# Rotary embedding in a two-layer attention kernel: partner rows by projection or by a row shuffle

## The chip, the cores and the metric

The kernel runs on one core of a Trainium2 chip. The metric is the device time of one execution in microseconds (us); the shown time is the median of three runs. The engines are TensorE (PE, with its weight loads as PEld), VectorE (DVE), ScalarE (ACT), GpSimd (POOL) and SyncE (SP), which issues the transfers.

## What is computed

Two layers over 64 sequences of 128 rows and 128 features, with 16 heads of 8 features. The first layer has a self-attention, a cross-attention to 77 context rows and an MLP; the second has one more cross-attention. Only the queries and keys of the self-attention are rotated:

```python
def _apply_rope(t, cos, sin):
    t1, t2 = jnp.split(t, 2, axis=-1)
    rot = jnp.concatenate([-t2, t1], axis=-1)
    return t * cos + rot * sin
...
t = (h @ qkv_W).reshape(b, n, 3, H, HD)
q, k, v = (t[:, :, 0], t[:, :, 1], t[:, :, 2])
return (_apply_rope(q, cos, sin), _apply_rope(k, cos, sin), v)
...
s = jnp.einsum('bqhd,bkhd->bhqk', q, k) * scale
a = jax.nn.softmax(s, axis=-1)
```

The first and the second 64 rows of a sequence carry the same positions, so a table of cosines or sines is 128 features by 64 columns. A feature's partner is the one four places further on in its head of eight, or four places back.

## The kernel before

Features lie on the partitions and rows (tokens) on the columns. Four sequences make a group of 512 columns; each of the three attentions has 16 groups, and a group has eight units (four sequences, two halves of the heads). The program is one long list of slots, a unit to a slot. On each engine the order within a slot is written out by hand; the class `Plan` gives the slots of the jobs that use the two PSUM banks `ps_pj`: projections ("q", "k", "v"), centring ("c") and mean square ("m") of the layer norm, and the output projection ("o"). A job's bank alternates with its place in the list, and the job two places before it must have been read first (`free_bank`).

In a slot of the self-attention PE does this, in order: at every second slot the transposition of the split maxima (L520, waits for POOL's L871); the mask products into both score banks (L491, wait for the row maxima of the slot before, L637, and for the exponentials, L815); the scores in natural order for the unit six ahead (L506); the transposed scores (L534); the value products of the unit before (L555); then the jobs that `Plan` calls late. L555 waits, in a slot with a transposition L520, for the copy L645 that DVE makes of what L520 wrote.

DVE in a slot: first the jobs of the slot before (the reads of `ps_pj`, L622 for the projections), then at every second slot the copy `mt` of the transposed maxima (L645), then the row maxima `negmax` over 1024 columns of PSUM (L637), then at every second slot five instructions that read out the values (L656 to L663; the last is a row shuffle over 128 columns).

Call b the slot in which PE projects the queries of a self-attention group. The jobs are q in slot b, the rotated query qr in b+1, k and the next group's c in b+2, the rotated key kr in b+3, m in b+4, o in b+5, v in b+6. qr and kr multiply by `wrot`, in which the four-feature halves of each head's columns of `wqkv` change places; the sine table carries the signs. DVE multiplies q by `cosq` and qr by `sinq` (the softmax scale is in both), one slot after PE each; k and kr go the same way with `cos` and `sin`. Both products of a pair lie in `part`; POOL adds them into `whole` (L885). From there ACT rounds the high part to bf16 (L750), POOL takes the rest and repeats the high part (L890, L891), and two more steps make the remaining bf16 parts (L755 on ACT, L897 and L898 on POOL), which SP sends to `stacks`.

In the set-up, ACT makes `wrot` with four copies (L175) and DVE makes `cosq` and `sinq` (L132, L133); PE's first instruction waits for `sinq`. Ahead of the first unit there are 28 slots of start-up, in which PE also transposes the incoming groups (L413, L416), each of which waits for its transfer.

## Time and profile before

| | |
|---|---|
| median of 3 runs | 1246.61 us (1243.92 to 1249.29) |
| the profiled execution | 1245.41 us, of which the span is 1243.6 us |
| mean granted TensorE clock | 0.96 of full speed |
| PE busy | 1070.5 us (86%) |
| DVE / ACT / POOL busy | 833.2 / 848.6 / 846.2 us (67% / 68% / 68%) |
| self-attention, from its first row maxima to its last output | about 97 to 475 us |

PE is the busiest engine, but the others stand at two thirds, and the four hand work to each other within every slot. So the shares alone do not tell which one sets the pace in a slot: that is read from the waits, in the order of time. In the rows, "[0.49 <-PE ps_nat L506]" behind an instruction means that its engine sat idle for 0.49 us before it and that PE's L506 ended that.

### The profile page before, as it was taken

The numbers are of one execution on the slowest core, as the hardware profiler recorded it, in microseconds if no ns is written. First come the engines' busy times: TensorE is split into PE (matmuls) and PEld (weight loads), VectorE is DVE, ScalarE is ACT, GpSimd is POOL, SyncE is SP. The second block draws the span as 40 slices with busy tenths as digits, with TensorE's granted clock in tenths as the row PEclk, the third lists the DMA queues.
The fourth block names the chain that finished last, engine by engine and source line by source line (L and its number), as shares of the span: only waits on it lengthen the run. The fifth ranks groups of instructions, "written<-read, shape, count | busy, mean of one in ns | idle before, by whom it ended". The sixth has DMA issues, their size and how long they took to land.

```text
span 1243.6 us, 42372 instructions
## 1 busy us (share of the span) xinstructions
PE 1070.5 (86%) x16230; PEld 612.6 (49%) x16230; DVE 833.2 (67%) x2198; ACT 848.6 (68%) x1527; POOL 846.2 (68%) x1799
## 2 busy tenths in 40 slices
PE   0677888898898988888898788999998999999987
PEld 0543444444444444555555455444443566666665
DVE  3336777887787877878888775223224687888875
ACT  0234666666656666888888777778876787888765
POOL 0048767767767866887788643466878787888742
PEclk9978999999999999999999987999999899999988
DMA  3266554564654554656666660000023566776761
GB/s 102 70 168 119 102 97 86 101 107 77 105 103 86 99 93 77 107 100 99 115 108 103 104 108 6 0 1 1 17 38 57 87 119 120 126 128 123 122 119 38
DMA packets 165242, 109.92 MB, mean 88 GB/s; under 512 B 42778, under 2 KB 164787, under 8 KB 165043
## 3 DMA queue, kind: packets, MB, share of 16 engines
q1 hardware_dynamic: 165042, 107.22, 48.2%
q8 instruction: 131, 2.15, 0.7%
q14 instruction: 69, 0.56, 0.1%
HBM read 9.08 MB, written 4.19 MB: 11 GB/s over the span
## 4 chain that ended last, share of the span: by engine, by line
PE 44%; POOL 12%; issue 11%; ACT 10%; SPq 9%; DMA 5%; DVE 5%; POOLq 0%; ACTq 0%; DVEq 0%
PE ps_po L555 7%; SPq L989 7%; ACT p L815 5%; PE ps_st L534 5%; PE ps_nat L506 4%; PE ps_st L567 4%; PE ps_pj L436 4%; PE ps_po L576 4%; PE ps_pj L453 4%; PE ps_pj L431 3%; DMA stacks<-mt 3%; DVE negmax L637 2%; PE ps_pj L444 2%; POOL whole L890 2%; POOL parts L891 2%
## 5 line engine op out<-in xcount | busy, mean ns | idle before, releaser
L637 DVE TENSOR_REDUCE negmax<-ps_nat 128x8 f32<-128x616 f32 (+1 forms) x384 | 359.8, 937 | 92.8 <-PE ps_nat L506 85.0
L815 ACT ACTIVATE p<-ps_st 128x1024 f32<-128x1024 f32 (+1 forms) x256 | 260.7, 1018 | 193.6 <-PE ps_st L534 192.5
L555 PE MATMUL ps_po<-p,vz 77*32 77x128 f32 (+1 forms) x6144 | 258.9, 288 | 3.5 <-ACT p L815 2.1
L534 PE MATMUL ps_st<-stacks 64*77 64x128 bf16 (+1 forms) x3072 | 157.9, 224 | 24.3 <-DMA stacks<-mt 13.1
L815 ACT ACTIVATE p<-ps_st,key_bias 77x1024 f32<-77x1024 f32 x128 | 141.8, 1108 | 50.9 <-PE ps_st L534 49.0
L555 PEld LDWEIGHTS ps_po<-p,vz 77*32 77x32 f32 (+1 forms) x6144 | 150.9, 112 | 43.4 <-issue 7.5
L506 PE MATMUL ps_nat<-stacks 64*128 64x77 bf16 (+1 forms) x3072 | 135.0, 210 | 26.4 <-issue 14.6
L879 POOL TENSOR_TENSOR ot<-vv,den 128x128 f32<-128x128 f32 x192 | 87.3, 455 | 102.5 <-ACT den L803 97.3
L506 PEld LDWEIGHTS ps_nat<-stacks 64*128 64x128 bf16 x3072 | 79.3, 97 | 151.9 <-issue 140.0
L890 POOL TENSOR_TENSOR whole<-whole,parts 128x512 f32<-128x512 f32 x96 | 98.6, 1027 | 57.1 <-ACT parts L750 57.0
L534 PEld LDWEIGHTS ps_st<-stacks 64*77 64x77 bf16 (+1 forms) x3072 | 107.5, 111 | 35.5 <-ACT p L815 27.9
L917 POOL TENSOR_TENSOR ht<-xc,nrm 128x512 f32<-128x512 f32 x48 | 60.9, 1268 | 75.8 <-ACT nrm L786 58.5
L645 DVE COPY mt<-ps_po 128x128 bf16<-128x128 bf16 x192 | 42.4, 221 | 100.7 <-PE ps_po L520 99.6
L898 POOL TENSOR_TENSOR parts<-whole,parts 128x512 bf16<-128x512 f32 x96 | 98.6, 1027 | 0.0
L891 POOL COPY parts<-parts 128x1024 bf16<-128x1024 bf16 x96 | 88.5, 922 | 0.0
L922 POOL TENSOR_SCALAR ht<-ht,mod 128x128 f32<-128x128 f32 x192 | 83.2, 448 | 5.0
L436 PE MATMUL ps_pj<-nrm,mean 128*128 128x512 f32 (+1 forms) x160 | 80.4, 599 | 5.2 <-ACT nrm L784 4.6
L685 DVE COPY xc<-ps_pj 128x512 f32<-128x512 f32 (+1 forms) x64 | 39.5, 631 | 51.5 <-PE ps_pj L431 51.2
L520 PE MATMUL ps_po<-eye_bf,nm 128*128 128x128 bf16 x192 | 43.8, 228 | 35.0 <-POOL nm L871 33.9
L656 DVE TENSOR_SCALAR dd<-ps_po,lower 128x128 f32<-128x128 f32 x192 | 65.6, 342 | 11.6 <-PE ps_po L555 11.6
L491 PE MATMUL ps_nat<-rolled,eye_bf 32*32 32x512 bf16 x1024 | 55.8, 389 | 17.4 <-ACT p L815 12.0
L431 PE MATMUL ps_pj<-xt,centre 128*128 128x512 f32 x128 | 70.0, 629 | 0.7 <-DVE xc L685 0.4
(146 smaller groups left out, 2139.8 us busy)
## 6 DMA issues: line engine op xcount, KB each, us to landing
stacks<-parts SPq DMA_DIRECT2D x512, 128.0 KB, 3.2
stacks<-parts SPq DMA_DIRECT2D x256, 77.0 KB, 2.8
stacks<-mt SPq DMA_DIRECT2D x192, 32.0 KB, 2.4
p<-in_x_dram SPq DMA_DIRECT2D x16, 256.0 KB
out_dram<-part SPq DMA_DIRECT2D x16, 256.0 KB, 2.3
p<-in_ctx_dram SPq DMA_DIRECT2D x16, 154.0 KB
stacks<-in_L_xcond_adaLN_W_dram SPq DMA_DIRECT2D x1, 576.0 KB
w<-in_L_xcond_mlp_W_dram SPq DMA_DIRECT2D x2, 256.0 KB
```

Of the source, the lines that this page charges most:

```text
L431: t.matmul(bank_of(job)[:, 0:w], c.centre[:], src[:, at:at + w], start=True, stop=True).then_inc(pj_full, 1)
L436: t.matmul(bank_of(job)[:, 0:w], c.mean[:], c.nrm[:, plan.norms[job[1]] % 3, 0:w], start=True, stop=True).then_inc(pj_full, 1)
L506: m = t.matmul(c.ps_nat[h][:, nk * g:nk * g + nk], qst[half(h), par, at, S * j:S * j + S], kst[half(h), par, at, nk * j:nk * j + nk], star ...
L534: m = t.matmul(c.ps_st[h][0:nk, S * g:S * g + S], kst[half(h), par, at, nk * j:nk * j + nk], qst[half(h), par, at, S * j:S * j + S], start ...
L555: m = t.matmul(c.ps_po[step % 2][32 * g:32 * g + 32, S * p:S * p + S], c.vz[0:nk, i % 2, step % G, g, at:at + 32], c.p[0:nk, hh, S * g:S * ...
L637: v.tensor_reduce(c.negmax[:, step % 2, :].rearrange("p (h q g) -> p h q g", h=2, q=2)[:, :, p, :], c.nat_pair[:].rearrange("p (h n) -> p ...
L815: a.activation(c.p[0:nk, 2 * p:2 * p + 2, :].rearrange("p h n -> p (h n)"), c.st_pair[0:nk, :], ACT.Exp, bias=bias).then_inc(exped, 1)
L879: p.tensor_tensor(c.ot[:, i % 2, S * j:S * j + S], c.vv[:, step % 2, :], c.den[:, step % 2, :], ALU.mult).then_inc(out_ready, 1)
L890: p.tensor_tensor(c.whole[:, x, w], c.whole[:, x, w], parts[:, hi[0], w], ALU.subtract).then_inc(rest, 1)
L891: p.tensor_copy(parts[:, hi[1]:hi[2] + 1:hi[2] - hi[1], w], parts[:, hi[0]:hi[0] + 1, w].broadcast_to([128, 2, width(i, x)]))
L898: p.tensor_tensor(parts[:, LOW[x], w], c.whole[:, x, w], parts[:, md[0], w], ALU.subtract).then_inc(split[x], 1)
L989: sp.dma_start(st[:, i % 3, t, 0:w], c.parts[16 * t:16 * t + 16, x, 6 * (i % 2):6 * (i % 2) + 8, 0:w]).then_inc(stacked[x][p][i % 3], 16)
```

## The change

The projections qr and kr are taken out, with `wrot` and ACT's four copies. DVE now reads the bank of q twice in one go: once times the cosine into `part`, once times the sine into `gated` (a tile that is otherwise used by the MLP). Then, behind a wait for that second product, it shuffles the rows of `gated` into the second half of `part`, so that each row gets the product of its partner. For this the sine table itself must be in shuffled order, which is one more shuffle (and one wait) in the set-up. POOL's addition waits for the shuffle instead of for the second projection's product.

```diff
+PARTNER_ROWS = [r ^ (HD // 2) for r in range(32)]
...
-            load(c.sin[:], ins["sin"])
+            load(c.sin_in[:], ins["sin"])
...
             v.tensor_scalar(c.cosq[:], c.cos[:], SCALE, None, ALU.mult)
+            v.stream_shuffle(c.sin[:], c.sin_in[:], PARTNER_ROWS).then_inc(shuffled, 1)
+            dve.wait_ge(shuffled, 1)
             v.tensor_scalar(c.sinq[:], c.sin[:], SCALE, None, ALU.mult).then_inc(ready, 1)
...
-            for x in range(2):
-                src = c.wqkv[:, D * x:D * x + D].rearrange("p (h t e) -> p h t e", t=2, e=4)
-                dst = c.wrot[:, x, :].rearrange("p (h t e) -> p h t e", t=2, e=4)
-                for t in range(2):
-                    a.activation(dst[:, :, t, :], src[:, :, 1 - t, :], ACT.Copy)
...
-            for kind, r in ((("q", 0), ("qr", 1), ("k", 2), ("kr", 3)) if i < NG else (("q", -1), ("k", 1))):
+            for kind, r in ((("q", 0), ("k", 2)) if i < NG else (("q", -1), ("k", 1))):
...
                 if a == 0:
-                    r = len(kind) - 1
                     if 2 * i + x > 0:
                         dve.wait_ge(turned, 2 * i + x)
-                    table = ((c.cosq, c.sinq), (c.cos, c.sin))[x][r]
-                    v.tensor_tensor(c.part[:, r, :].rearrange("p (r n) -> p r n", n=64),
-                                    bank[:].rearrange("p (r n) -> p r n", n=64),
-                                    table[:].unsqueeze(1).broadcast_to([128, 8, 64]), ALU.mult).then_inc(taken, 1)
+                    blocks = lambda tile: tile.rearrange("p (r n) -> p r n", n=64)
+                    for table, dst in zip(((c.cosq, c.sinq), (c.cos, c.sin))[x], (c.part[:, 0, :], c.gated[:, x, :])):
+                        m = v.tensor_tensor(blocks(dst), blocks(bank[:]), table[:].unsqueeze(1).broadcast_to([128, 8, 64]), ALU.mult)
+                    m.then_inc(taken, 1)
+                    dve.wait_ge(taken, plan.taken[job])
+                    v.stream_shuffle(c.part[:, 1, :], c.gated[:, x, :], PARTNER_ROWS).then_inc(rotated, 1)
...
             def turn(i, x):
-                pool.wait_ge(taken, plan.taken["qk"[x] + "r", i])
+                pool.wait_ge(rotated, 2 * i + x + 1)
```

How this moves instructions, first on PE. The place is slots b and b+1 of a self-attention group: `wqkv` with `ht` is the projection q, `wrot` the projection qr. Before:

```order
L555 MATMUL ps_po<-p,vz 32x128 x8
L453 MATMUL ps_pj<-ht,wqkv 128x512
L520 MATMUL ps_po<-eye_bf,nm 128x128
L491 MATMUL ps_nat<-rolled,eye_bf 32x512 x2
L491 MATMUL ps_st<-rolled,eye_bf 32x512 x2
...
L506 MATMUL ps_nat<-stacks 128x128 x8
L534 MATMUL ps_st<-stacks 128x128 x8
L555 MATMUL ps_po<-p,vz 32x128 x8
L453 MATMUL ps_pj<-ht,wrot 128x512
L491 MATMUL ps_nat<-rolled,eye_bf 32x512 x2
```

And now (line numbers are one or two lower):

```order
L554 MATMUL ps_po<-p,vz 32x128 x8
L452 MATMUL ps_pj<-ht,wqkv 128x512
L519 MATMUL ps_po<-eye_bf,nm 128x128
L490 MATMUL ps_nat<-rolled,eye_bf 32x512 x2
L490 MATMUL ps_st<-rolled,eye_bf 32x512 x2
...
L505 MATMUL ps_nat<-stacks 128x128 x8
L533 MATMUL ps_st<-stacks 128x128 x8
L554 MATMUL ps_po<-p,vz 32x128 x8
L490 MATMUL ps_nat<-rolled,eye_bf 32x512 x2
```

The value products of slot b+1 are now followed at once by the mask products of slot b+2; slot b+3 changes in the same way.

On DVE, slots b+1 to b+3 of a group. Before:

```order
L622 TENSOR_TENSOR part<-ps_pj,cosq 128x512
L645 COPY mt<-ps_po 128x128
L637 TENSOR_REDUCE negmax<-ps_nat 128x2x4
...
L663 STREAM_SHUFFLE den<-dd 128x128
L622 TENSOR_TENSOR part<-ps_pj,sinq 128x512
L637 TENSOR_REDUCE negmax<-ps_nat 128x2x4
L622 TENSOR_TENSOR part<-ps_pj,cos 128x512
L645 COPY mt<-ps_po 128x128
L637 TENSOR_REDUCE negmax<-ps_nat 128x2x4
```

Now:

```order
L621 TENSOR_TENSOR part<-ps_pj,cosq 128x512
L621 TENSOR_TENSOR gated<-ps_pj,sinq 128x512
L624 STREAM_SHUFFLE part<-gated 128x512
L645 COPY mt<-ps_po 128x128
L637 TENSOR_REDUCE negmax<-ps_nat 128x2x4
...
L663 STREAM_SHUFFLE den<-dd 128x128
L637 TENSOR_REDUCE negmax<-ps_nat 128x2x4
L621 TENSOR_TENSOR part<-ps_pj,cos 128x512
L621 TENSOR_TENSOR gated<-ps_pj,sin 128x512
L624 STREAM_SHUFFLE part<-gated 128x512
L645 COPY mt<-ps_po 128x128
L637 TENSOR_REDUCE negmax<-ps_nat 128x2x4
```

The sine product has moved forward by one slot, and it and the shuffle now stand ahead of the copy `mt` and of the row maxima of slot b+1 (and again of b+3); slots b+2 and b+4 have lost a product.

## Rows read from the trace of the kernel before

**Rows 1.** The page's first part: busy time, share of span, instructions, by engine.
```profile
PE 1070.5 (86%) x16230; PEld 612.6 (49%) x16230; DVE 833.2 (67%) x2198; ACT 848.6 (68%) x1527; POOL 846.2 (68%) x1799
```

**Rows 2.** Busy time by stretch: length, then PE, PEld, DVE, ACT, POOL, clock, DMA.
```profile
240.00:300.00 60.00, 52.84 (x1048) 28.09 (x1050) 47.31 (x111) 36.38 (x69) 45.42 (x91) 1.00 0.59 103
```

**Rows 3.** Timeline, POOL: L890 for the queries, groups 4 and 15 of 16.
```profile
135.78 1.16 POOL L890 TENSOR_TENSOR whole<-whole,parts 128x512 f32<-128x512 f32 x1 [3.96 <-ACT parts L750]
...
398.61 1.16 POOL L890 TENSOR_TENSOR whole<-whole,parts 128x512 f32<-128x512 f32 x1 [3.96 <-ACT parts L750]
```

**Rows 4.** Timeline, PE, one period: start, duration, engine, line, what, idle before.
```profile
245.42 0.23 PE L520 MATMUL ps_po<-eye_bf,nm 128*128 128x128 bf16 x1 [0.36 <-POOL nm L871]
...
246.49 0.64 PE L555 MATMUL ps_po<-p,vz 128*32 128x128 f32 x16
247.07 1.12 PE L453 MATMUL ps_pj<-ht,wrot 128*128 128x512 f32 x2
248.12 0.39 PE L491 MATMUL ps_nat<-rolled,eye_bf 32*32 32x512 bf16 x2
...
253.08 1.12 PE L453 MATMUL ps_pj<-ht,wrot 128*128 128x512 f32 x2
...
258.42 0.23 PE L520 MATMUL ps_po<-eye_bf,nm 128*128 128x128 bf16 x1 [1.67 <-POOL nm L871]
```

**Rows 5.** Timeline, the other engines, the same period.
```profile
245.09 0.69 DVE L622 TENSOR_TENSOR part<-ps_pj,cosq 128x512 f32<-128x512 f32 x1 [0.46 <-PE ps_pj L453]
...
245.70 0.21 DVE L645 COPY mt<-ps_po 128x128 bf16<-128x128 bf16 x1
...
246.41 1.22 DVE L637 TENSOR_REDUCE negmax<-ps_nat 128x8 f32<-128x1024 f32 x1 [0.49 <-PE ps_nat L506]
...
249.55 1.27 POOL L885 TENSOR_TENSOR whole<-part 128x512 f32<-128x512 f32 x1 [0.80 <-DVE part L622]
...
255.24 1.16 POOL L890 TENSOR_TENSOR whole<-whole,parts 128x512 f32<-128x512 f32 x1 [3.96 <-ACT parts L750]
```

**Rows 6.** By line: count, then ns least/median/most, first and last start, forms.
```profile
L663 DVE STREAM_SHUFFLE den<-dd x192: 289/294/302, 123.6 to 1235.9; 128x128 f32<-128x128 f32 x192
...
L685 DVE COPY xc<-ps_pj x64: 466/680/692, 401.0 to 1153.3; 128x512 f32<-128x512 f32 x48, 128x308 f32<-128x308 f32 x16
...
L164 DVE COPY bp_rows<-ps_pj x1: 292/292/292, 44.9 to 44.9; 128x128 f32<-128x128 f32 x1
```

**Rows 7.** Timeline, set-up.
```profile
33.47 0.27 PE L184 MATMUL ps_pj<-eye,stacks 25*128 25x25 f32 x1 [33.47 <-DVE sinq L133]
...
34.71 0.19 DVE L139 TENSOR_SCALAR stacks<-stacks 128x64 f32<-128x64 f32 x1 [0.32 <-ACT stacks L177]
...
34.94 0.55 DVE L141 RECIPROCAL stacks<-stacks 128x64 f32<-128x64 f32 x1
```

**Rows 8.** Timeline, DVE and PE's weight loads, slots b+1 and b+2 of the last group.
```profile
413.57 0.69 DVE L622 TENSOR_TENSOR part<-ps_pj,cosq 128x512 f32<-128x512 f32 x1 [0.60 <-PE ps_pj L453]
...
414.35 1.23 DVE L637 TENSOR_REDUCE negmax<-ps_nat 128x8 f32<-128x1024 f32 x1
...
416.16 0.09 PEld L491 LDWEIGHTS ps_nat<-rolled,eye_bf 32*32 32x32 bf16 x2 [0.76 <-DVE negmax L637]
```

**Rows 9.** Timeline, PE, start-up.
```profile
66.93 2.00 PE L453 MATMUL ps_pj<-ht,wrot 128*128 128x512 f32 x2
...
79.70 0.66 PE L413 MATMUL ps_st<-eye,p 128*128 128x128 f32 x4 [2.83 <-DMA p<-in_ctx_dram]
...
105.67 2.07 PE L453 MATMUL ps_pj<-ht,wrot 128*128 128x512 f32 x2
```

**Rows 10.** A timeline row of PE, then two stretches (columns as in Rows 2).
```profile
465.60 0.23 PE L520 MATMUL ps_po<-eye_bf,nm 128*128 128x128 bf16 x1 [1.67 <-POOL nm L871]
...
465.00:468.00 3.00, 2.18 (x49) 1.30 (x50) 1.63 (x4) 1.02 (x1) 2.87 (x6) 0.77 0.71 129
552.00:555.00 3.00, 3.00 (x26) 1.32 (x30) 1.89 (x7) 1.96 (x4) 1.94 (x5) 0.50 0.44 69
```

More of the change, by code:

```diff
@@ L50, in setup_phase @@
                                                  s("su_silu_d"), s("su_copied"))
-    headed = s("su_headed")
+    headed, shuffled = s("su_headed"), s("su_shuffled")
     made, masks, mask_ps = s("su_made"), s("su_masks"), s("su_mask_ps")
@@ L322, in by_dve @@
     def by_dve(self, job):
-        return job[0] in ("q", "qr", "k", "kr", "o") or job[0] == "c" and not self.copied_by_act(job[1])
+        return job[0] in ("q", "k", "o") or job[0] == "c" and not self.copied_by_act(job[1])
     @staticmethod
@@ L336, in main_phase @@
     rooted, multiplied, applied = s("rooted"), s("multiplied"), s("applied")
+    rotated = s("rotated")
     turned, high, rest, mid = s("turned"), s("high"), s("rest"), s("mid")
@@ L362, in main_phase @@
     width = lambda i, x: NT if x == 0 else G * keys(i)
-    weights = [{"q": c.wqkv[:, 0:D], "k": c.wqkv[:, D:2 * D], "v": c.wqkv[:, 2 * D:3 * D], "qr": c.wrot[:, 0, :], "kr": c.wrot[:, 1, :]},
+    weights = [{"q": c.wqkv[:, 0:D], "k": c.wqkv[:, D:2 * D], "v": c.wqkv[:, 2 * D:3 * D]},
                {"q": c.w0[:, 0, :], "k": c.w0[:, 1, :], "v": c.w0[:, 2, :]},
@@ L1044, in two_layers @@
         c.wqkv = sb("wqkv", [D, 3 * D])
-        c.wrot = sb("wrot", [D, 2, D])
+        c.sin_in = sb("sin_in", [128, 64])
         c.w0 = sb("w0", [D, 3, D])
```

## The prediction

> **What bounds the kernel now.** The page first: PE is the busiest engine, the others stand at two thirds [rows 1]. That does not say that PE sets the pace, so the stretch in which the change lives comes next: between 240 and 300 us PE is busy 52.84 of 60 us at full clock, DVE 47.31, POOL 45.42 [rows 2]. Nobody is full; the pace is a cycle through several engines. How regular it is shows in POOL's L890: from the fourth to the fifteenth group it comes from 135.78 to 398.61 us, 11 periods of 23.89 us [rows 3]. So one period, followed link by link, gives the self-attention.
>
> I read the period around 245 us backwards from its longest PE wait. At 258.42 PE has waited 1.67 us for POOL's L871 (slot b+5) [rows 4]. POOL is late because L890 started only at 255.24, after 3.96 us of waiting for ACT's L750 [rows 5]; that stands behind the exponentials of slot b+3, which wait for PE's scores of that slot. PE reaches slot b+3 without any wait once the mask products of b+2 have started at 248.12, and these start when the projection qr (247.07) has left PE [rows 4]. So up to b+3 the start of PE's work is what counts, and behind b+3 PE has 1.67 us in hand.
>
> **The change, part by part.** All times are those of the period in [rows 4, 5].
>
> *Taking qr off PE (slot b+1).* Without it PE could start the mask products of b+2 as soon as the row maxima of b+1 are there: they start at 246.41, take 1.22 and end at 247.63; PE follows about 0.06 later, at 247.69. Before it was 248.12. The most that this removal can give is 0.43 us a group, not the 1.05 us that the projection holds PE.
>
> *What DVE does instead.* q is there at 245.09, as before. A 512-column product releases the next instruction after 0.61 (245.09 to 245.70), so the sine product runs from 245.70 to 246.39. Then comes the wait for its own result. Instructions that don't wait start about 0.08 before the end of the one before; where DVE waits for its own result, as from L139 (ends 34.90) to L141 (34.94), it starts 0.04 after the end [rows 7]. So the shuffle starts at 246.43.
>
> How long is a 128x512 shuffle? The trace has only 128x128: 0.294 [rows 6]. A copy grows from 0.292 at 128 columns to 0.692 at 512 [rows 6], 0.400 for 384 columns; with the same growth the shuffle takes 0.69. Its ends are 0.29 (width costs nothing) and 4 x 0.294 = 1.18 (no fixed part). I take 0.69, since the two instructions cost the same at 128 columns. The shuffle ends at 247.12.
>
> The copy `mt` then runs from 247.04 to 247.25, where it was at 245.70, and the row maxima from 247.17 to 248.39. Two engines wait for these. PE's value products L555 wait for `mt` and start at 247.31 instead of 246.49; they end in time. The mask products of b+2 wait for the maxima and start at 248.45 instead of 248.12. **So slot b+1 costs 0.33 us a group more, not 0.43 less.** With a shuffle of 0.29 it would be 0.07 less than before, with 1.18 it would be 0.82 more.
>
> By the Trainium skill, "VectorE: DVE Perf Modes", the perf-mode tier table, a row shuffle has only the 1x rate, about 2400 ns at 2048 columns; a quarter of that is an estimate of 0.60 us here. With it the cost would be 0.24 a group instead of 0.33. The same page, "The DRAIN you can't avoid", says that a semaphore between Vector instructions costs nothing extra. The trace disagrees (0.08 before the end against 0.04 after it); by the page the cost would be lower by 0.12 a group.
>
> *Slot b+2.* DVE has lost a product there, which had hidden behind PE. POOL's addition L885 waited 0.80 for qr's product [rows 5]; now the shuffle is early, but POOL first splits the maxima that come 0.76 later (247.63 to 248.39), takes 1.06 for that, and starts L885 at 249.45 instead of 249.55. Nothing waits for the 0.10.
>
> *Slots b+3 and b+4: kr.* k is ready at 251.11 (values from 249.37, 0.58 for them, 1.16 for the projection as for q). Cosine product, sine product, wait and shuffle take 2.03, so `mt` is copied at 253.06, the value products start at 253.33, the maxima end at 254.41, and the mask products of b+4 start at 254.47 instead of 254.13 (before: behind kr, 253.08 plus 1.05). That is 0.34 late, which is no more than the 0.33 brought along: the loss in this slot is covered by kr's going. And behind it lies PE's wait of 1.67 [rows 4]. If that cover were gone, its full price is about what b+1 costs.
>
> *Period.* L750, L890 and the transposition in b+5 all come 0.33 later; b+5 to b+8 have no edit. Twelve groups (the fourth to the fifteenth): 12 x 0.33 = **+4.0**.
>
> *The last group* has no next group to centre, and DVE runs closer behind PE: its maxima start 0.78 after the q product (413.57 to 414.35) without a wait [rows 8], where in the period there are 1.32. They now start at 415.65 and end at 416.87, and PE's next slot starts at 416.93 instead of 416.16 [rows 8]: **+0.8**.
>
> *Set-up.* PE's first instruction waits for `sinq` [rows 7]. Ahead of it stand one shuffle of 64 columns (0.23 by the same growth) and a wait (0.04): **+0.3**. ACT's four copies hid beside this.
>
> *Start-up.* Six rotated projections lie here, some at the half clock, 2.00 and 2.07 long [rows 9]. Together they are at most 6 x 2.07 = 12.4, at least nothing. Most of what they free is given back to the transfers: PE waits for the input again and again, 2.83 us at 79.70 [rows 9], and each input is requested only when an earlier one has been transposed. Only the one at 105.67 has no such wait behind it, and the shuffles take part of that back. I take half of that one: **-1.0**.
>
> *Sum:* 4.0 + 0.8 + 0.3 - 1.0 = +4.1 on the profiled execution's 1245.4: 1249.5. That execution lies 1.2 below the median of the runs, so for a median I say **1250.7**.
>
> **The rivals.**
>
> *The clock falls more often (slower).* PE gets emptier: in b+1 it now idles some 0.8 ahead of the value products and 0.6 behind them, and in b+3 and b+4 again 0.5 and 0.6, with the 1.67 us still there. In the twelve periods no such gap lowered the clock, but the same gap at 465.60 was followed by a granted clock of 0.77 and then 0.67 (the 1.2 GHz level in part of the stretch), and in the cross-attention there are stretches of 3 us wholly at 0.50, that is at 1.2 GHz [rows 10]. In 3 us at half clock and 3.00 busy, PE does 1.5 us less. Two to six falls more: +3 to +9, 1254 to 1260. Against it: the gap itself gets no longer.
>
> *The cover in b+3 fails (slower).* If DVE's late maxima in b+3 reach the exponentials or POOL, each group pays about 0.33 twice: +4 to +5 more, 1255. It decides from 1.67 us of lateness in b+4, and I count 0.34. Weak.
>
> *The start-up gives more (faster).* If no transfer waits for what PE no longer does, the six projections are worth up to 12.4 and half of them, 6.2, would give 1245.4 + 1.2 + 5.1 - 6.2 = 1245.5; with a short shuffle as well (0.29: -0.07 instead of +0.33 a group) 1240.7. By the full 12.4 and the forecast shuffle it is 1239.3, which is faster. Against it: the waits for transfers.
>
> *The edit does nothing.* If PE's 1.05 and DVE's addition cancelled in every slot, 1246.6. It takes a shuffle of about 0.36, half of what I take.
>
> **How the numbers follow.** Forecast (1247.5 to 1253.5): 0.50. More clock falls: 0.27. Cover fails, or a shuffle towards 1.18 (12 x 0.49 = +5.9): 0.08. No effect: 0.08. Start-up gain: 0.07. The range leaves out the far ends of the first rival and the larger start-up gains: 1244 to 1260. A measurement of this kernel can tell 0.5% from no change, 6.2 us: slower begins at 1252.8. Slower: most of the falls (0.24), the failing cover (0.07) and the forecast's upper edge (0.08), 0.39. Faster: 0.05. Same: 0.56.
>
> **What would show it.** In the changed profile: STREAM_SHUFFLE 128x512 at 0.69; the sine product 0.61 behind the cosine; PE's mask products in b+2 waiting for L637 instead of following a projection; L890's period at 24.2; PE's wait for L871 in b+5 still near 1.6; L885 no longer waiting for DVE; PE's clock at 1.00 between 120 and 450 us. A period of 23.9 or less, or one of 24.6, makes the sum wrong; so does a start of the periods (135.8) that moves by more than 2 us.

## The result and the profile after

The changed kernel takes **1273.99 us** (median of 4 runs, 1267.11 to 1279.98), the kernel before in the same session 1246.92 (1243.92 to 1249.29): ratio 1.0217, 95% interval 1.0159 to 1.0274. It is slower by 2.2%, 27 us, where +4.1 had been forecast, and it lies outside the range. The interval is clear of no change, but it doesn't say whether the loss is more than 2%. The profiled execution took 1279.98 us with a span of 1278.2, 34.6 more than the span of before; it is the slowest of the four.

The first part of the page of after, to be held against [rows 1]:

```profile
PE 1069.3 (84%) x16166; PEld 618.9 (48%) x16166; DVE 853.4 (67%) x2264; ACT 848.8 (66%) x1523; POOL 849.0 (66%) x1799
```

PE has lost 64 matmuls and hardly any busy time (1069.3 for 1070.5). The projections that went were paid back by slower ones elsewhere: the mean clock fell from 0.960 to 0.932. So the place to look is the clock by stage. Stretches of before, then of after (length, busy time and instructions of PE, PEld, DVE, ACT, POOL, then PE's granted clock, DMA share, GB/s). In both they are: the start-up, up to the fourth group's L890; the 11 periods; the last groups of the self-attention; the cross-attention and what overlaps it; the rest:

```profile
0.00:135.80 135.80, 80.14 (x742) 47.82 (x746) 62.38 (x124) 37.92 (x75) 49.67 (x84) 0.92 0.49 116
135.80:398.60 262.80, 229.34 (x4516) 122.73 (x4512) 204.99 (x481) 165.47 (x309) 196.58 (x385) 1.00 0.55 96
398.60:443.00 44.40, 38.30 (x737) 20.32 (x729) 34.90 (x81) 29.31 (x55) 37.03 (x74) 1.00 0.52 96
443.00:723.80 280.80, 245.08 (x4478) 143.94 (x4482) 226.30 (x655) 223.34 (x407) 212.63 (x499) 0.97 0.60 101
723.80:1243.60 519.80, 477.64 (x5777) 277.81 (x5777) 304.63 (x860) 392.52 (x683) 350.31 (x761) 0.94 0.40 70
```
```profile
0.00:137.90 137.90, 75.08 (x726) 47.44 (x730) 67.46 (x142) 37.24 (x71) 49.70 (x83) 0.89 0.48 113
137.90:417.30 279.40, 223.01 (x4472) 123.84 (x4468) 218.32 (x526) 166.13 (x309) 196.97 (x386) 0.94 0.51 90
417.30:464.60 47.30, 38.98 (x733) 20.86 (x725) 36.05 (x85) 29.26 (x55) 37.19 (x73) 0.93 0.51 90
464.60:751.80 287.20, 250.03 (x4478) 145.71 (x4482) 226.36 (x655) 223.52 (x407) 213.72 (x500) 0.95 0.59 99
751.80:1278.20 526.40, 482.19 (x5777) 281.02 (x5773) 305.18 (x860) 392.69 (x683) 351.46 (x761) 0.93 0.39 69
```

Taken from L890 to L890, the difference of 34.6 is +2.2 in the start-up, +16.5 in the 11 periods, +3.0 in the last groups, +6.3 in the cross-attention and +6.6 in the rest. In the first three the change has its edits; the code of the last two is the same in both kernels.

**One period, as forecast.** The timeline of after, slot b+1 of a group in which the clock stayed at 1.00 (start, duration, engine, line, what, idle before); the rows answer to [rows 4, 5]:

```profile
177.91 0.69 DVE L621 TENSOR_TENSOR part<-ps_pj,cosq 128x512 f32<-128x512 f32 x1 [0.46 <-PE ps_pj L452]
178.51 0.68 DVE L621 TENSOR_TENSOR gated<-ps_pj,sinq 128x512 f32<-128x512 f32 x1
179.24 0.72 DVE L624 STREAM_SHUFFLE part<-gated 128x512 f32<-128x512 f32 x1
179.85 0.21 DVE L645 COPY mt<-ps_po 128x128 bf16<-128x128 bf16 x1
179.97 1.22 DVE L637 TENSOR_REDUCE negmax<-ps_nat 128x8 f32<-128x1024 f32 x1
180.21 0.64 PE L554 MATMUL ps_po<-p,vz 128*32 128x128 f32 x16 [0.79 <-DVE mt L645]
181.25 0.09 PEld L490 LDWEIGHTS ps_nat<-rolled,eye_bf 32*32 32x32 bf16 x2 [0.66 <-DVE negmax L637]
182.47 1.27 POOL L885 TENSOR_TENSOR whole<-part 128x512 f32<-128x512 f32 x1
191.57 0.23 PE L519 MATMUL ps_po<-eye_bf,nm 128*128 128x128 bf16 x1 [1.70 <-POOL nm L871]
```

Everything stands where the working put it. Counted from the cosine product, the sine product starts 0.60 later, `mt` 1.94, the maxima 2.06, the mask products 3.34 (worked out: 0.61, 1.95, 2.08, 3.36). L885 waits for nobody, and the long wait in b+5 is 1.70.

**Three periods.** The same for POOL's L890 (queries) of four groups in a row, as in [rows 3], and what stands in the last of the three periods: two waits of PE with a row of PE between them, and four stretches of 3 us (columns as above):

```profile
188.37 1.16 POOL L890 TENSOR_TENSOR whole<-whole,parts 128x512 f32<-128x512 f32 x1 [3.96 <-ACT parts L750]
212.59 1.16 POOL L890 TENSOR_TENSOR whole<-whole,parts 128x512 f32<-128x512 f32 x1 [3.96 <-ACT parts L750]
236.82 1.16 POOL L890 TENSOR_TENSOR whole<-whole,parts 128x512 f32<-128x512 f32 x1 [3.96 <-ACT parts L750]
263.75 1.16 POOL L890 TENSOR_TENSOR whole<-whole,parts 128x512 f32<-128x512 f32 x1 [5.10 <-ACT parts L750]
```
```profile
240.02 0.23 PE L519 MATMUL ps_po<-eye_bf,nm 128*128 128x128 bf16 x1 [1.69 <-POOL nm L871]
251.54 0.22 PE L519 MATMUL ps_po<-eye_bf,nm 128*128 128x128 bf16 x1
254.04 0.65 PE L554 MATMUL ps_po<-p,vz 128*32 128x128 f32 x16 [1.36 <-DVE mt L645]
```
```profile
240.00:243.00 3.00, 2.98 (x51) 1.46 (x51) 2.21 (x6) 1.74 (x3) 3.00 (x4) 0.80 0.05 11
243.00:246.00 3.00, 3.00 (x51) 1.60 (x51) 2.79 (x9) 1.76 (x3) 2.67 (x7) 0.63 0.41 62
253.00:256.00 3.00, 1.56 (x44) 1.10 (x46) 2.96 (x11) 0.77 (x1) 0.68 (x4) 0.91 0.18 39
256.00:259.00 3.00, 3.00 (x28) 1.65 (x25) 1.40 (x4) 1.53 (x3) 1.84 (x3) 0.52 0.86 158
```

The first two periods are 24.22 and 24.23, and 24.22 had been forecast. The third is 26.93. In it PE waits 1.69 at 240.02, and from 241.8 to 245.1 it has the 1.2 GHz level; it waits 1.36 for `mt` at 254.04, and has 1.2 GHz again from 255.4 to 258.9. The second wait is a new one: it lies in the slot in which DVE now has the shuffle ahead of `mt`. It is longer here than the 0.79 of 180.21 although the clock is back at 1.00. The first fall has delayed PE, so POOL's L871 is now ready in time: at 251.54 PE doesn't wait for it, where it waits 0.39 one group earlier (226.72). PE so reaches the copy sooner, and DVE's way to the copy is as long as before (2.30 from the cosine product to L554, both times). The two falls cost 2.71 together, 1.36 each on the average. Of the 11 periods six have the forecast length, one costs 2.0 more and four cost 2.7 more: 11 x 0.33 = 3.6 for the lateness and 12.9 for the clock, 16.5 together.

**All runs, by their clock.** Each run comes with its mean granted clock. The 82 other runs of the kernel before that accompanied the experiments have 0.943 to 0.969, median 0.955 at a span of 1246.8; the time at half clock is twice the span times (1 - clock), 112 us in the median run. Over these 82 runs the span grows by 0.31 us for each us at half clock. The four of after have 0.932 to 0.943, median 0.936, 162 us at half clock: 50 us more, at 0.31 each 15.5. The median span is 25.4 longer; 4 to 5 of it are the forecast lateness, and the some 5 left are not placed. In after's 11 periods a us at half clock cost more, 0.38 (12.9 for 34). This is an estimate, from how the runs of before spread; by it the larger part of the loss is clock over the runs too, not only in the profiled one.

### The profile page after: what moved, and what is told of

Its sections match the earlier page's. It is cut to its first block, busy times and chain, and to the rows that moved or that the text cites. A ratio compares the mean times of both kernels' runs of the same rounds, so it can differ in the third digit from the quotient of the medians.

```text
span 1278.2 us, 42276 instructions
## 1 busy us (share of the span) xinstructions
PE 1069.3 (84%) x16166; PEld 618.9 (48%) x16166; DVE 853.4 (67%) x2264; ACT 848.8 (66%) x1523; POOL 849.0 (66%) x1799
## 4 chain that ended last, share of the span: by engine, by line
PE 48%; ACT 11%; issue 11%; SPq 8%; DVE 7%; POOL 6%; DMA 5%; POOLq 0%; DVEq 0%; ACTq 0%
PE ps_po L554 9%; ACT p L815 6%; SPq L989 6%; PE ps_st L533 5%; PE ps_nat L505 5%; PE ps_pj L452 4%; PE ps_st L566 4%; PE ps_pj L435 4%; PE ps_po L575 4%; PE ps_pj L430 4%; PE ps_pj L443 3%; DMA stacks<-mt 3%; DVE negmax L637 2%; PE ps_nat L490 2%; POOL whole L890 2%
## 5 line engine op out<-in xcount | busy, mean ns | idle before, releaser
L554 PE MATMUL ps_po<-p,vz 77*32 77x128 f32 (+1 forms) x6144 | 266.1, 294 | 23.7 <-DVE mt L645 22.3
L554 PEld LDWEIGHTS ps_po<-p,vz 77*32 77x32 f32 (+1 forms) x6144 | 155.6, 114 | 66.8 <-issue 24.5
L533 PE MATMUL ps_st<-stacks 64*77 64x128 bf16 (+1 forms) x3072 | 162.6, 228 | 25.7 <-DMA stacks<-mt 14.8
L505 PE MATMUL ps_nat<-stacks 64*128 64x77 bf16 (+1 forms) x3072 | 138.1, 213 | 27.2 <-issue 15.2
L890 POOL TENSOR_TENSOR whole<-whole,parts 128x512 f32<-128x512 f32 x96 | 98.7, 1028 | 68.1 <-ACT parts L750 67.9
L533 PEld LDWEIGHTS ps_st<-stacks 64*77 64x77 bf16 (+1 forms) x3072 | 111.0, 114 | 36.6 <-ACT p L815 23.5
L490 PE MATMUL ps_nat<-rolled,eye_bf 32*32 32x512 bf16 x1024 | 57.2, 402 | 29.6 <-DVE negmax L637 16.5
L865 POOL CAST nm<-negmax 128x16 bf16<-128x16 f32 x192 | 37.9, 197 | 53.2 <-DVE negmax L637 52.6
```

The source lines that it names most:

```text
L505: m = t.matmul(c.ps_nat[h][:, nk * g:nk * g + nk], qst[half(h), par, at, S * j:S * j + S], kst[half(h), par, at, nk * j:nk * j + nk], star ...
L533: m = t.matmul(c.ps_st[h][0:nk, S * g:S * g + S], kst[half(h), par, at, nk * j:nk * j + nk], qst[half(h), par, at, S * j:S * j + S], start ...
L554: m = t.matmul(c.ps_po[step % 2][32 * g:32 * g + 32, S * p:S * p + S], c.vz[0:nk, i % 2, step % G, g, at:at + 32], c.p[0:nk, hh, S * g:S * ...
L890: p.tensor_tensor(c.whole[:, x, w], c.whole[:, x, w], parts[:, hi[0], w], ALU.subtract).then_inc(rest, 1)
```

## The experiments

The theory: the change puts idle time of PE into b+1 and b+3 (ahead of and behind the value products), and with it the clock falls behind PE's longer waits. Rivals: the gap in b+5 alone does it (then filling b+1 and b+3 helps nothing); the shuffle's place ahead of the maxima does it; the changed spacing of the waits (the period) does it.

"Filling" means products that compute nothing that is used. They go into the PSUM bank of the job that comes next:

```diff
+            def fill(slot, place):
...
+                for _ in range(n[place]):
+                    t.matmul(bank_of(job)[:, 0:192], weights[0]["q"], ht(i)[:, 0:192], start=True, stop=True)
...
+                fill(slot, 0)
                 if val is not None:
                     values(val)
...
+                fill(slot, 1)
```

The table has all kernels: "falls" are the drops of the clock that begin between 120 and 430 us of the profiled execution (the 11 periods end at 395 to 417, so a fall can lie behind them), "11 periods" their length and clock in it; then come the median clock of all runs, the median time and the ratio to the runs of before on the same chip.

| kernel | period | falls | 11 periods | clock in them | clock, all runs | us | ratio (95%) |
|---|---|---|---|---|---|---|---|
| before (a second profile: c_before_again) | 23.89 | 0 (0) | 262.8 (262.9) | 1.00 | 0.955 | 1246.9 | 1 |
| after | 24.22 | 9 | 279.3 | 0.94 | 0.936 | 1274.0 | 1.022 (1.016 to 1.027) |
| a_fill13 | 24.27 | 1 | 267.7 | 0.99 | 0.948 | 1263.1 | 1.011 (1.004 to 1.019) |
| a_fillall | 24.26 | 0 | 266.6 | 1.00 | 0.954 | 1258.2 | 1.006 (1.003 to 1.010) |
| b_fillgap | 24.21 | 2 | 265.7 | 1.00 | 0.948 | 1262.7 | 1.012 (1.005 to 1.019) |
| a_noshuffle | 23.57 | 7 | 265.6 | 0.96 | 0.944 | 1256.6 | 1.005 (1.002 to 1.008) |
| a_late | 23.60 | 5 | 262.1 | 0.98 | 0.944 | 1256.8 | 1.004 (1.001 to 1.007) |
| b_latefill | 23.58 | 1 | 259.4 | 1.00 | 0.948 | 1253.1 | 1.005 (1.002 to 1.008) |
| b_longer | 24.75 | 4 | 273.4 | 0.98 | 0.950 | 1263.9 | 1.014 (1.007 to 1.021) |
| b_beforegap | 23.89 | 0 | 262.8 | 1.00 | 0.954 | 1251.2 | 1.003 (0.999 to 1.007) |
| c_before_delay | 24.16 | 5 | 267.7 | 0.97 | 0.952 | 1253.6 | 1.008 (1.005 to 1.010) |
| c_late_delay | 24.17 | 7 | 271.1 | 0.96 | 0.937 | 1266.2 | 1.018 (1.014 to 1.021) |
| d_late_delay1 | 23.89 | 1 | 263.1 | 0.99 | 0.952 | 1252.4 | 1.000 (0.997 to 1.004) |
| c_latefill_start | 23.58 | 0 | 259.6 | 1.00 | 0.960 | 1249.3 | 1.002 (0.999 to 1.005) |
| d_before_once | 23.89 | 0 | 262.9 | 1.00 | 0.953 | 1252.4 | 1.002 (0.999 to 1.005) |
| d_before_start | 23.89 | 0 | 262.9 | 1.00 | 0.962 | 1248.6 | 1.001 (0.997 to 1.004) |

### Filling PE's new idle time, and the old gap

a_fill13 is after with one product of 192 columns ahead of and one behind the value products in b+1 and b+3. a_fillall has three more at the end of b+4, ahead of the long wait. b_fillgap has only these three.

> The changed kernel, with small matrix products given back to TensorE where it now waits: in slots b+1 and b+3 of each self-attention group one product of 192 columns ahead of the value products and one behind them (32 x 2 products of about 0.4 us; their results are overwritten unread, the output is the same). Clock theory (most of the loss comes from the clock's falls, which the emptier TensorE brings on): the falls that follow slot b+1 go, those behind the 1.7 us wait in b+5 may stay; 1252 to 1262. Latency theory (the shuffle ahead of the copy mt and of the row maxima is what costs, and the falls only go with it): no gain, 1270 or more. Undisturbed periods 24.2 to 24.3 under both.

> As the run before, and in addition three products of 192 columns (about 1.2 us) behind the last job of slot b+4, that is in the 1.7 us for which TensorE waits for L871 in b+5 (for groups 1 to 14). Clock theory: hardly any fall is left between 120 and 450 us, periods of 24.2 to 24.4 throughout, 1246 to 1254. Latency theory: 1270 or more.

> The changed kernel with the wait of 1.7 us in b+5 filled alone (three products of 192 columns) and slots b+1 and b+3 left empty. Which of the empty places brings the falls: if the long wait is enough alone, no fall is left between 120 and 450 us and the time is that with everything filled, 1254 to 1260. If the emptiness of b+1 and b+3 brings them by itself, four or more are left, behind b+1: 1262 to 1270.

The 11 periods of the three, in this order:

```profile
139.40:407.20 267.80, 231.69 (x4560) 130.38 (x4564) 217.39 (x526) 165.56 (x309) 196.31 (x386) 0.99 0.54 94
```
```profile
137.60:404.20 266.60, 241.17 (x4622) 141.24 (x4621) 216.99 (x525) 165.49 (x308) 196.35 (x385) 1.00 0.54 95
```
```profile
137.90:403.60 265.70, 219.98 (x4538) 128.22 (x4534) 216.96 (x526) 165.46 (x309) 196.26 (x385) 1.00 0.54 95
```

With more for PE to do, each stretch is 12 to 14 us shorter than in after, and the clock is back. 266.6 is 11 x 24.22 = 266.4 and nothing else: the lateness that was forecast, without the clock. Either filling alone is nearly enough in the profiled execution (one fall left, and two, both of which begin behind the 11 periods), so neither gap is the sole cause. Over the runs, a_fillall brings the ratio from 1.022 down to 1.006, but its 1258.2 lies above the 1246 to 1254 that the clock theory had expected. The span of its profiled execution is 13.0 above that of before: 3.8 of it in the periods, 1.8 in the start-up, 0.8 in the last groups, and 6.6 in the cross-attention and the rest, whose code is the same. The other two stay at 1.011 and 1.012 with wide intervals (4 runs each); b_fillgap's profiled execution lost in the cross-attention (293.0 for before's 280.8), in code that no edit touches.

### The shuffle left out, and the shuffle behind the maxima

a_noshuffle leaves the shuffle out: POOL adds the sine product as it is, so the partner rows are the wrong ones. PE's work is that of after.

```diff
-                    for table, dst in zip(((c.cosq, c.sinq), (c.cos, c.sin))[x], (c.part[:, 0, :], c.gated[:, x, :])):
+                    for table, dst in zip(((c.cosq, c.sinq), (c.cos, c.sin))[x], (c.part[:, 0, :], c.part[:, 1, :])):
...
-                    dve.wait_ge(taken, plan.taken[job])
-                    v.stream_shuffle(c.part[:, 1, :], c.gated[:, x, :], PARTNER_ROWS).then_inc(rotated, 1)
...
-                pool.wait_ge(rotated, 2 * i + x + 1)
+                pool.wait_ge(taken, plan.taken["qk"[x], i])
```

a_late keeps it, with its wait, but issues it behind the row maxima of the slot:

```diff
                     maxima(unit_at(slot + AHEAD))
+                for job in coming:
+                    if job[0] in "qk" and job[1] < NG:
+                        shuffle_partners(job)
```

> The changed kernel without the partner shuffle and its wait: the sine product goes straight into the second half of part, so the rotation adds the wrong rows' products (the output is not the reference's). Latency theory: the maxima of b+1 start at their old time, undisturbed periods 23.5, and the time is below before: 1238 to 1244. Clock theory: undisturbed periods are 23.5 as well, but TensorE is as empty as in the changed kernel and waits just as long in b+5, so falls still come, 4 or more between 120 and 450 us: 1246 to 1262.

> The changed kernel with the shuffle moved on VectorE from ahead of the copy mt to behind the row maxima of the same slot. Both theories: undisturbed periods of 23.5 to 23.9, since the maxima of b+1 start at 246.45 instead of 247.17 (in the times of the period shown) and the read-out behind them has time. Latency theory: 1238 to 1246. Clock theory: falls still come as without the shuffle, 1246 to 1262.

The order on DVE in a_late, then the 11 periods of a_noshuffle and of a_late:

```profile
181.10 1.22 DVE L640 TENSOR_REDUCE negmax<-ps_nat 128x8 f32<-128x1024 f32 x1
182.25 0.73 DVE L633 STREAM_SHUFFLE part<-gated 128x512 f32<-128x512 f32 x1
```
```profile
136.20:401.70 265.50, 216.32 (x4468) 121.25 (x4464) 203.64 (x481) 164.75 (x309) 196.42 (x385) 0.96 0.53 95
```
```profile
136.10:398.20 262.10, 212.24 (x4471) 119.73 (x4464) 215.98 (x526) 164.66 (x309) 196.80 (x386) 0.98 0.55 96
```

The shuffle and its wait off the path are worth 24.22 - 23.57 = 0.65 a period, and moving them is worth as much as leaving them out (23.60). That settles the forecast's own mechanism: DVE ahead of the maxima is the path. But the clock falls all the same (7 and 5 times), and a_noshuffle gives back 6.2 of the 7.1 us that it had won in these periods. So the clock needs neither the shuffle nor its wait for its falls; what these two kernels share with after is the emptier PE and a period other than 23.89. One thing is new in them: PE's wait for L871 in b+5 is 1.99 to 2.00 where it is 1.70 in after.

### Late shuffle with filling, and the gap filled in the kernel before

b_latefill is a_late with one product behind the value products in b+1 and b+3 and three at the end of b+4. b_beforegap is before with the three alone.

> The changed kernel with the shuffle behind the row maxima, and fills behind the value products of b+1 and b+3 (one product of 192 columns each) and behind the last job of b+4 (three). Clock theory: periods of 23.6 to 23.7 without a fall between 120 and 450 us: 5 to 8 us below the late shuffle alone, 1249 to 1252, at or a little below before in the same runs. Latency theory: like the late shuffle alone, 1256.

> The kernel before with three matrix products of 192 columns behind the last job of slot b+4, in TensorE's wait of 1.7 us for L871 (groups 1 to 14). Clock theory: the profiled run of before had no fall between 120 and 450 us, so its own profile gains nothing in the self-attention (periods 23.9); over the runs, whose spread would come from falls, the median may fall by 0 to 4 us. If the fill delays anything, periods of 24 and a median 1 to 3 us higher.

Their 11 periods, in this order:

```profile
136.50:395.90 259.40, 230.56 (x4582) 135.24 (x4574) 215.50 (x525) 164.35 (x309) 196.35 (x385) 1.00 0.56 97
```
```profile
133.90:396.70 262.80, 239.98 (x4582) 133.99 (x4578) 204.98 (x481) 165.40 (x309) 196.58 (x385) 1.00 0.55 96
```

In b_latefill these periods are 3.4 us shorter than in before, 0.31 each, which is what the change can give here once its two costs are gone. The whole is not: 1253.1, ratio 1.005. The clock theory had expected 1249 to 1252, and 5 to 8 us less than with the late shuffle alone; that missed, since a_late has the ratio 1.004 and the intervals of the two lie over each other. So the filling that brings the clock back in these periods shows no gain over the runs here, and only the profiled stretch speaks for it. The cross-attention took 291.1 in the profiled execution, and the median clock of all ten runs is 0.948. In before, whose clock did not fall in these periods, the three products change nothing, as they should.

### Spacing of the waits, or emptiness of PE

Two theories are held against each other: that the falls come because PE has lost work and waits more often (emptiness), or because its long waits no longer come every 23.89 us (spacing). Only DVE is given more to do in these, in slot b+6, ahead of the maxima. b_longer is before with a copy of 512 columns, c_before_delay is before with two shuffles of 256 columns into an idle tile, c_late_delay is a_late with the same two, and d_late_delay1 is a_late with one of 320 columns, chosen to come back to before's period.

```diff
+                if 2 <= slot <= NG * PER - LEAD - 2 and (slot + LEAD) % PER == 6:
+                    for n in range(2):
+                        v.stream_shuffle(c.gated[:, n, 0:256], c.mod[:, 0:4, :].rearrange("p m n -> p (m n)")[:, 0:256], DEN_ROWS)
                 if unit_at(slot + AHEAD) is not None:
                     maxima(unit_at(slot + AHEAD))
```

> The kernel before, its projections untouched, with one more VectorE copy (128x512, about 0.4 us, into a tile idle at the time) ahead of the row maxima of slot b+6 in each self-attention group: the period gets about as long as in the changed kernel (24.2 to 24.3 instead of 23.89) while TensorE keeps all its work. Emptiness theory (the falls come because TensorE lost work and waits more often): no falls, or one or two, between 120 and 450 us; 14 or 15 times 0.35 us, 5 us above before. Period theory (it is enough that the waits of 1.7 us in b+5 no longer come every 23.89 us; some of them then meet the clock's watch unfavourably): four or more falls, 10 us or more above before.

> The kernel before with two more row shuffles of 256 columns on VectorE (into a tile idle at the time) ahead of the row maxima of slot b+6, in the groups whose period was measured. TensorE keeps all its projections; of the 0.7 us some 0.4 should vanish in a wait for the exponentials and for L871 that is there already (as 1.28 us became 0.86 in the run with a copy), so the period becomes 24.1 to 24.2, near that of the changed kernel (24.22). Emptiness theory: no or one fall between 130 and 420 us, periods undisturbed, 3 to 5 us above before. Period theory (the period's length alone decides whether the waits of 1.7 us in b+5 make the clock fall): four or more falls there, 6 to 12 us above before.

> The counterpart: the changed kernel with the shuffle behind the row maxima (TensorE as empty as in the changed kernel, periods of 23.60) and the same two shuffles in b+6: period 23.85 to 23.92, that of the kernel before. Emptiness theory: falls as with the late shuffle alone (6 between 120 and 450 us) or more. Period theory: none or one between 160 and 400 us, since the waits come at the spacing that had none in the kernel before.

> The changed kernel with the late shuffle and one more row shuffle of 320 columns (0.42 us of VectorE) in b+6: of the 0.70 us added before, 0.57 reached the period, so of 0.42 some 0.29 should: a period of 23.87 to 23.91, that of the kernel before, with the emptier TensorE. Spacing theory (what counts is the time from one long wait to the next, 23.89 being a good one): no or one fall between 170 and 400 us. Emptiness theory: five or more.

The 11 periods of c_before_delay, c_late_delay and d_late_delay1:

```profile
135.50:403.20 267.70, 234.01 (x4514) 125.34 (x4509) 212.44 (x525) 165.65 (x309) 196.71 (x385) 0.97 0.53 94
```
```profile
136.00:407.10 271.10, 217.14 (x4472) 121.81 (x4464) 223.93 (x571) 164.81 (x309) 196.40 (x386) 0.96 0.53 93
```
```profile
134.70:397.80 263.10, 209.54 (x4468) 118.11 (x4464) 219.94 (x548) 164.22 (x309) 196.38 (x386) 0.99 0.54 96
```

These four sort by two properties:

| | PE as full as before | PE emptier |
|---|---|---|
| period 23.89 | 0 falls (before, twice; d_before_once; d_before_start) | 1 fall, at 140 (d_late_delay1) |
| period 24.16 to 24.22 | 5 falls (c_before_delay) | 7 (c_late_delay), 9 (after) |

The first column is the strongest result of the study: PE's instructions are the same in before and in c_before_delay and the wait in b+5 is 1.67 in both, yet with 0.27 more from one wait to the next there are five falls in place of none. So the falls need neither work taken off PE nor a longer wait. Over the runs c_before_delay is 7.5 us above before on the same chip, about half of which are its 14 longer periods (14 x 0.27 = 3.8).

Two things keep the column from being a clean test of spacing. Three waits of PE in c_before_delay show them:

```profile
138.72 0.23 PE L520 MATMUL ps_po<-eye_bf,nm 128*128 128x128 bf16 x1 [1.67 <-POOL nm L874]
...
162.60 0.23 PE L520 MATMUL ps_po<-eye_bf,nm 128*128 128x128 bf16 x1 [1.67 <-POOL nm L874]
...
218.27 0.39 PE L491 MATMUL ps_nat<-rolled,eye_bf 32*32 32x512 bf16 x2 [0.96 <-DVE negmax L637]
```

DVE's two shuffles also lengthen another wait: in b+7 PE waits 0.96 for the maxima, where before waits 0.26. No fall begins behind it; four of the five begin 0.5 to 1.9 us after the end of the wait in b+5, and the last one behind a wait of 0.81. And the first two falls, at 139.2 and 163.1, stand behind waits that end 23.88 apart, though DVE's extra shuffles begin at 117.80. So a spacing of 23.89 is no safeguard as such: here a fall came twice running at that spacing, while in the four profiles with a period of 23.89 none came behind any of the waits in b+5. Whether the spacing counts, or where the waits lie in time, which a spacing of 23.89 may only keep as it is, these runs don't separate.

The second row is weaker: emptiness adds falls, and c_late_delay's median clock is 0.937 where c_before_delay's is 0.952. And d_late_delay1, in which DVE does 0.52 us more work a group than in a_late, has falls at the old spacing only at 140, and a median clock of 0.952 where a_late has 0.944; its time is that of before, though its interval and a_late's overlap. Its wait in b+5 is 1.99, so that longer wait alone doesn't make the falls either. c_late_delay's period came out 24.17 where 23.88 had been expected of it, so it landed in the row of after and not in that of before; that is why d_late_delay1 was run. b_longer misses too, as an experiment: its copy took 1.36, not the some 0.4 for which it was chosen, its wait in b+7 grew to 1.54, and its period became 24.75, with four falls.

What makes 23.89 a good period, if it is one, was not found. It isn't that shorter is better: at 23.57 and 23.60, with PE emptier, there are 7 and 5 falls.

### The start-up, and what comes later

c_latefill_start is b_latefill with two products of 192 columns more in each of 20 slots of the start-up; d_before_start is before with these alone; d_before_once is before with two shuffles of 512 columns in b+6 of two late groups, so that the cross-attention begins later; c_before_again is before.

> The late shuffle with fills in the self-attention as in the run with both, and two products of 192 columns in each slot of the start-up from the first projection on (20 slots). Clock theory: the falls at 62, 79 and 103 us (24 us at half clock in the profile without these fills) get shorter or go, the periods begin 2 to 4 us earlier (133 to 135 instead of 136.5), 1248 to 1252. If the start-up is bound by its transfers anyway: no change, 1253.

> The kernel before with two products of 192 columns in each of the 20 start-up slots from the first projection on, nothing else. Clock theory: fewer or shorter falls before 110 us (15 to 22 us at half clock in the two profiles of before), the periods start 0 to 2 us earlier, and the self-attention has no falls: 1242 to 1247, at or a little below before. If the moment at which the later stages start decides, that may eat it up.

> The kernel before, in which two slots near the end of the self-attention (b+6 of two groups) get two row shuffles of 512 columns each ahead of the row maxima, 1.2 us of which about 0.8 reach the end of the period; everything else is as before. If the moment at which the cross-attention starts decides on the falls there, the stretch from the first to the last L890 behind the self-attention takes 284 us or more instead of 281 to 282, and the median is 5 to 10 us above before. If it does not, only the 1.6 us show.

> The kernel before once more, unchanged, for a second profile: how much its cross-attention and MLP (280.8 us from the first to the last L890 behind the self-attention in the first profile, where seven other kernels with the same code there took 285 to 293) vary from one execution to the next. Clock theory: 281 to 293 us with a different set of falls, and the difference follows the time at half clock.

The start-up and the cross-attention of d_before_start:

```profile
0.00:133.80 133.80, 84.05 (x826) 57.10 (x830) 62.48 (x124) 37.88 (x75) 49.74 (x84) 1.00 0.50 117
...
441.00:729.10 288.10, 252.10 (x4478) 146.80 (x4482) 226.36 (x655) 223.03 (x407) 212.85 (x500) 0.94 0.59 98
```

The filled start-up keeps the clock at 0.99 (c_latefill_start) and 1.00. What it gains is small: 133.8 for 135.8 in the first profile of before (the second has 132.7 without it), 135.2 for 136.5 in b_latefill. In d_before_start the cross-attention then lost 7.3 against the first profile of before, so the median didn't move. The version with everything, c_latefill_start, is level with before (0.9993 to 1.0048), and no version was faster than before beyond its interval.

Left open: what sets the clock in the cross-attention. It took 280.8 and 282.3 us in the two profiles of before, and 283 to 293 in every other kernel, with the same code. A late start of it, tried in d_before_once (285.5), doesn't tell: the ratio is 1.0021 (0.9994 to 1.0048). Since the runs of before alone spread from 0.943 to 0.969 in clock, two profiles of it don't show what is usual there. So of the 34.6 us the last 12.9 are seen as clock (0.97 to 0.95, and 0.94 to 0.93), but not tied to the change.

## Why the prediction was wrong

Point by point:

- **The shuffle at 0.69, bounds 0.29 and 1.18.** The 32 of after, by line (count, then ns least/median/most): 0.72, close to the copy's growth that it was taken from [rows 6].

```profile
L624 DVE STREAM_SHUFFLE part<-gated x32: 716/720/730, 69.5 to 441.0; 128x512 f32<-128x512 f32 x32
```

The estimate of 0.60 that the prediction takes from the Trainium skill, "VectorE: DVE Perf Modes", the perf-mode tier table, was too low by a sixth.

- **The wait for the own result.** The sine product ends at 179.19, the shuffle starts at 179.24, 0.05 behind it (taken: 0.04). The statement of the Trainium skill, "VectorE: DVE Perf Modes", "The DRAIN you can't avoid", that a semaphore between Vector instructions costs nothing extra (measured there on a row of copies), does not hold in this trace either: the instruction that waits for nothing starts 0.09 before such an end (178.51 against 178.60).
- **Slots b+1 to b+4, the period.** Right: 24.22, the cover in b+3 holds, L885 is free, the wait in b+5 is 1.70. Moving the shuffle gave 0.62 a period, which confirms that DVE ahead of the maxima is the path in b+1.
- **Set-up +0.3.** The two instructions cost what was said, but PE's first one didn't move, 33.48 now. DVE's chain ahead of it began 0.26 earlier, at 32.53 where it was 32.79, with the landing of the mask. Here are the rows that answer to [rows 7]:

```profile
32.89 0.21 DVE L134 STREAM_SHUFFLE sin<-sin_in 128x64 f32<-128x64 f32 x1
33.14 0.20 DVE L136 TENSOR_SCALAR sinq<-sin 128x64 f32<-128x64 f32 x1
33.48 0.27 PE L182 MATMUL ps_pj<-eye,stacks 25*128 25x25 f32 x1 [33.48 <-DVE sinq L136]
```

- **Start-up -1.0.** Wrong in sign: +2.2. The clock over it is 0.89 where it was 0.92; some 31 us of it are at the 1.2 GHz level where 20 were. One pair of profiles says little here, but the sign holds: six profiles with before's start-up reach the fourth group's L890 at 132.7 to 136.5, the four with after's at 137.6 to 139.5. The working treated the six projections as time to be won. That PE waits for the transfers anyway, and with less to do between them spends longer at 1.2 GHz, fits but isn't shown: with the shuffle late or left out and no filling of the start-up the same point comes at 134.7 to 136.5, though the six projections are gone there as well.
- **Last group +0.8.** It came to +3.0 in after, with two falls. In a_fillall, whose clock holds until the last 0.2 us of this stretch, it is +0.8 (45.2 for 44.4), as forecast; so the term was right and the other 2.2 stand beside the clock.
- **"PE's clock at 1.00 between 120 and 450".** This is the step that failed: the sum takes the clock as unchanged and holds no term for it. It was named as a sign to look for, the mechanism was the first rival, and both its chance (0.27) and its size (two to six falls, +3 to +9) were too small: 9 falls up to 430 and two more up to 450, 12.9 us in the periods alone, beside the start-up and the last groups. The argument against it was "the gap itself gets no longer". That is true, 1.70 for 1.67, and it decides nothing: c_before_delay has the same gap and the same PE program and falls five times, with 0.27 more from one gap to the next. With the gaps filled (a_fillall) the periods come to 266.6 where the forecast's 24.22 gives 266.4, so what the sum left out there was the clock. The prediction also counted idle time in b+1 and b+3 but not what it becomes behind a fall: PE, delayed, no longer waits for L871 ahead of it, the wait for `mt` grows from 0.79 to 1.36, and a second fall follows the first. Why the clock falls behind some of these waits and not behind others stays open, and so do the 12.9 us behind the self-attention. In after's waits of PE between 140 and 410 us (us in total, times, longest) it stands second, and in before it is not in the list:

```profile
PE ps_po L519 <- POOL nm L871: 21.0, 17, 1.7
PE ps_po L554 <- DVE mt L645: 16.6, 21, 1.4
```

The rival that the cover in b+3 fails, the one that the start-up gives more, and the one that nothing happens all fell with the measured period and the +2.2.

## What to carry to other kernels

Work taken off TensorE is worth the time by which its next start moves, here 0.31 of 1.05 us a group once the shuffle was out of the way (b_latefill), and it can cost clock: if a loop stands at full clock with a wait in every period, don't take that for granted when the period or the filling changes, and price either with the falls that it may bring (here from nothing to 1.5 us each, up to two a period). To find out which it is, put products that compute nothing into the waits: if the loop returns to the length worked out from the rows, the rest was clock. And put a dependent instruction whose result isn't needed yet behind the one that TensorE waits for, even if both are short: that was 0.62 us a group.

## What the runs showed of the hardware

- **The same wait may lower the clock or not.** With TensorE's program unchanged and its wait in b+5 unchanged at 1.67 us, four profiles with a period of 23.89 us have no fall between 120 and 430 us, and c_before_delay, whose period is 24.16, has five, one of them behind a wait of 0.81. A fall in the periods cost 1.36 us on the average in after, 1.16 in a_fill13, 0.5 to 1.0 in c_before_delay, and two of those in b_longer (at 214 and 313) nothing.
- **Shuffle by width.** A row shuffle on VectorE from SBUF takes 0.294 us at 128 columns, 0.449 at 256 (c_before_delay), 0.518 at 320 (d_late_delay1), 0.72 at 512.
- **A copy held up by GpSimd.** b_longer's copy of 512 columns took 0.42 to 1.37 us. Three of them from DVE's timeline, then POOL's operation that runs beside the second and the third:

```profile
142.52 0.42 DVE L725 COPY gated<-eye 128x512 f32<-128x512 f32 x1
...
167.38 1.37 DVE L725 COPY gated<-eye 128x512 f32<-128x512 f32 x1
...
217.19 1.03 DVE L725 COPY gated<-eye 128x512 f32<-128x512 f32 x1
```
```profile
167.19 1.27 POOL L919 TENSOR_TENSOR ht<-xc,nrm 128x512 f32<-128x512 f32 x1
...
216.68 1.27 POOL L919 TENSOR_TENSOR ht<-xc,nrm 128x512 f32<-128x512 f32 x1
```

The first runs beside two small POOL operations, of which the one that begins under it (L871 of that kernel) takes 0.43 where it takes 0.20 at 166.73. The other two end 0.29 and 0.27 behind the end of L919 (168.75 against 168.46, 218.22 against 217.95), however late in it they began: as if the copy got on only when GpSimd's product of two SBUF operands is done. The Trainium skill, "Trainium Architecture — The Big Picture", "What this means for kernel authors", names the port pair shared by VectorE and GpSimd as an exclusive lock, and this trace agrees. The shuffles that stand in the same place in c_before_delay show nothing of the kind (437 to 463 ns, 28 of them).
